# Row additions in pieces, closer search rounds, packed list operands, constant products between the waits, and ternary side work in later tiles

## The reference, cut to what matters

```
prob = softmax(z @ gate)              # layer 0: 2048 x 8
per expert: the 256 largest of prob[:, e]; x[tok] += tanh(g) * prob * expert(z[tok])
x += tanh(g) * shared(z)
```

## Time and profile before

| | |
|---|---|
| median of 3 executions | 921.93 us (921.6 to 922.6) |
| the profiled execution | 921.86 us, span 920.1 us |
| TensorE matmul busy | 835.7 us, 91% of the span |
| VectorE, ScalarE, GpSimd busy | 454.9, 325.4, 206.7 us |
| mean granted TensorE clock | 0.975 of full speed |

### The profile page before, as it was taken

The page is one execution under the profiler, slowest core; times in us unless marked ns, Lnnn a source line. Parts: engine busy times, 40 slices in busy tenths (PEclk is TensorE's granted clock), DMA queues, the critical chain, the costliest instruction groups (busy, mean ns, idle before and its releaser), DMA issues. The chain is left out here.

```text
span 920.1 us, 15092 instructions
## 1 busy us (share of the span) xinstructions
PE 835.7 (91%) x5798; PEld 646.3 (70%) x5806; DVE 454.9 (49%) x1240; ACT 325.4 (35%) x628; POOL 206.7 (22%) x226
## 2 busy tenths in 40 slices
PE   7899899999999997899999999888899996499996
PEld 5675665678888875666676667665677775388886
DVE  2674755400132317577676766755888776100000
ACT  2335022112322223555454545546455432122121
POOL 0123600020424310001000101111756124212222
PEclk9999899999999999999999999999999997599999
DMA  6032800014646447000000000000000002436351
GB/s 230 24 126 81 324 26 23 24 28 181 226 151 196 114 118 262 1 2 1 1 2 1 2 1 1 2 1 1 1 1 2 24 35 81 138 104 205 126 179 21
DMA packets 33873, 70.58 MB, mean 77 GB/s; under 512 B 9218, under 2 KB 23946, under 8 KB 28939
## 3 DMA queue, kind: packets, MB, share of 16 engines
q1 hardware_dynamic: 26937, 59.92, 18.2%
q0 software_dynamic: 6144, 8.31, 4.7%
q10 hardware_dynamic: 722, 1.39, 0.4%
HBM read 54.98 MB, written 14.80 MB: 76 GB/s over the span
## 5 line engine op out<-in xcount | busy, mean ns | idle before, releaser
L604 PE MATMUL banks<-arena 32*120 32x256 f32 (+6 forms) x1808 | 161.6, 377 | 15.9 <-DVE small L1965 12.6
L1262 ACT ACTIVATE arena<-banks 128x512 f32<-128x512 f32 (+4 forms) x185 | 106.8, 596 | 148.8 <-PE banks L1053 33.5
L604 PEld LDWEIGHTS banks<-arena 32*120 32x120 f32 (+5 forms) x1808 | 101.1, 163 | 51.7 <-issue 33.0
L604 PE MATMUL banks<-ffw,arena 128*128 128x256 bf16 (+2 forms) x632 | 120.0, 344 | 0.5 <-issue 0.2
L604 PE MATMUL banks<-arena,ew 128*128 128x256 f32 x512 | 115.6, 385 | 1.4 <-ACT arena L1262 1.4
L604 PE MATMUL banks<-ew,arena 128*128 128x256 f32 x512 | 113.2, 379 | 0.0
L604 PEld LDWEIGHTS banks<-arena,ew 128*128 128x128 f32 x512 | 98.9, 194 | 15.6 <-ACT arena L1262 2.0
L604 PEld LDWEIGHTS banks<-ew,arena 128*128 128x128 f32 x512 | 96.4, 190 | 12.3
L604 PEld LDWEIGHTS banks<-ffw,arena 128*128 128x128 f16 (+1 forms) x640 | 86.6, 138 | 25.2 <-issue 2.7
L1965 DVE TENSOR_REDUCE small<-banks 128x16 f32<-128x1920 f32 x32 | 69.0, 2157 | 20.8 <-PE banks L604 20.7
L1456 ACT ACTIVATE arena<-banks,mcol 120x2048 f32<-120x2048 f32 x32 | 63.1, 1971 | 19.0 <-PE banks L604 19.0
(11 more groups left out here) (242 smaller groups left out, 1237.4 us busy)
## 6 DMA issues: line engine op xcount, KB each, us to landing
ew<-in_w SPq DMA_DIRECT2D x32, 1024.0 KB, 7.1
xrow<-arena SPq DMA_DIRECT2D x1, 2064.0 KB, 22.0
arena<-xrow SPq DMA_DIRECT2D x8, 258.0 KB, 4.2
zrow<-arena SPq DMA_DIRECT2D x8, 256.0 KB, 2.2
ffw<-in_shared SPq DMA_DIRECT2D x2, 1024.0 KB, 6.0
acc<-x SPq DMA_DIRECT2D x4, 512.0 KB, 2.9
ffw<-in_tern SPq DMA_DIRECT2D x2, 1024.0 KB, 7.8
out<-x SPq DMA_DIRECT2D x8, 256.0 KB, 2.0
```

Source lines behind the costliest of these rows:

```text
L604: return pe.matmul(o, l, r, start=a, stop=b)
L1262: return nc.scalar.activation(o, i_, ACT.Copy)
```

## The change

- The bias row is added to `x` tile by tile, the addition of tile t after comparison t + 1; the later GpSimd work of `prepare_later` is cut and spread over rounds in the same way.
- Rounds are 4.5 units apart (30 + 9r // 2), and the list and its turn come two units later behind the last round.
- `hi1`, `lo1`, `lo2` and the digits are stored tile by tile, so that a tile's 128 columns lie side by side; the comparison with `iotaA` then repeats each digit as the innermost element. `add_shared(4)` comes behind the list's operands.
- `fill(bank, n)` issues n f32 products of 128 columns of a constant matrix of ones into a bank that is not in use: 15, 4 and 12 at the start, 6 in the first gate, 8, 14, 18 and 12 in the last gate, 40 and 22 behind its last ranks, the 22 after the moves have landed.
- The side steps of the last two batches move from ahead of the ternary tiles into tiles 4 to 10; GpSimd's `weigh` is split, and `weigh(1)` and `weigh(2)` come earlier.

The diff (context cut):

```
...
 XROW = D + 2
+FILL = {0: {0: 6}, 3: {5: 8, 6: 14, 7: 18}}
...
 def round_at(r):
-    return 30 + 5 * r
+    return 30 + 9 * r // 2
...
         c.at = 0
-        lo2 = c.take(16 * P, "p (m t) -> p m t", dt=F16, t=NT)
+        lo2 = c.take(16 * P, "p (t m) -> p t m", dt=F16, t=NT)
...
         c.at = 17344
-        iotaA = c.take(16 * NT, "p (a t) -> p a t", dt=F16, a=16)
+        iotaA = c.take(16, dt=F16)
...
         c.at = 18432
-        hi1 = c.take(16 * P, "p (m t) -> p m t", dt=F16, t=NT)
-        lo1 = c.take(16 * P, "p (m t) -> p m t", dt=F16, t=NT)
+        hi1 = c.take(16 * P, "p (t m) -> p t m", dt=F16, t=NT)
+        lo1 = c.take(16 * P, "p (t m) -> p t m", dt=F16, t=NT)
...
         posi = c.take(3 * P, "p (a n) -> p a n", dt=I32, a=3)
-        digit = c.take(2 * P, "p (a e t) -> p a e t", dt=F16, a=2, e=E)
+        digit = c.take(2 * P, "p (a t e) -> p a t e", dt=F16, a=2, e=E)
...
         su = sems("setup", "AB_ps AB_sb M_ps M_sb tanh gsum_in gsum_ps gsum_out pick16 parts later "
-                           "wT_ps wT_sb B_ps B_sb col_ps col_sb row_ps row_sb krow tern trow_ps trow_sb")
+                           "wT_ps wT_sb B_ps B_sb col_ps col_sb row_ps row_sb krow consts tern trow_ps trow_sb")
...
             g.memset(tri[:, :], 1.0)
-            g.drain()
+            g.drain().then_inc(su["consts"], 1)
...
                 g.drain().then_inc(su["later"], 1)
-                g.wait_ge(sh["cmp"], 1)
-                for i in range(T // 512):
-                    g.wait_ge(gt["z"], 2 * i + 2)
-                    xt = x[:, 4 * i:4 * i + 4, :]
-                    g.tensor_tensor(xt, xt, bcast(r, 1, 4), ALU.add).then_inc(su["later"], 1)
-                g.tensor_copy(iotaA[:, :, :], bcast(iota16[:, :], 2, NT))
+                for t in range(NT):
+                    g.wait_ge(sh["cmp"], t + 1)
+                    m = g.tensor_tensor(x[:, t, :], x[:, t, :], r, ALU.add)
+                    if t % 4 == 3:
+                        m.then_inc(su["later"], 1)
+                g.wait_ge(sh["cmp"], NT + 1)
+                g.tensor_copy(iotaA, iota16[:, :])
...
                 g.wait_ge(su["pick16"], 1)
-                g.tensor_copy(pick[:, :, :], bcast(pick16, 2, SK))
+                for a in range(4):
+                    g.wait_ge(sh["cmp"], NT + 2 + a)
+                    g.tensor_copy(pick[:, 4 * a:4 * a + 4, :], bcast(pick16[:, 4 * a:4 * a + 4], 2, SK))
...
                 for n, t_ in (("o1", 1), ("f1", 5), ("o2", 2)):
+                    g.wait_ge(sh["cmp"], NT + 6 + t_ // 2)
...
                     g.tensor_tensor(hw[:, t % 2], h2[:, t % 2], wrow, ALU.mult).then_inc(f2["hw"], 1)
+
+                def spread(t):
...
                 weigh(0)
-                rstd_side(UN - 1)
                 weigh(1)
-                add_bias(NB - 2)
+                spread(0)
                 weigh(2)
-                add_bias(NB - 1)
+                spread(1)
+                spread(2)
...
                     weigh(t)
+                    spread(t)
+                    if t == 5:
+                        rstd_side(UN - 1)
+                    elif t == 6:
+                        add_bias(NB - 2)
+                    elif t == 8:
+                        add_bias(NB - 1)
...
+            def fill(bank, n):
+
+                for _ in range(n):
+                    mm(bank[:, 0:P], onesf[:, :], onesf[:, :], True, True)
+
...
+            pe.wait_ge(su["consts"], 1)
+            fill(psum[7], 15)
...
                 turn_weights(psum[2 + a], n)
+            fill(psum[7], 4)
...
                 def gate_turn(k):
-                    pe.wait_ge(gt["z"], b0 + k + 1)
...
                         pe.wait_ge(gt["zT_sb"], b0 + k)
+                    fill(psum[6 if L == 0 else 2], FILL[L].get(k, 0))
+                    pe.wait_ge(gt["z"], b0 + k + 1)
...
                     w = t1 - t0
-                    pe.wait_ge(gt["picked"], n + 1)
...
                     pe.wait_ge(one["pT_sb"], b0 + (6 if n == 0 else NB))
+                    if n == 3:
+                        fill(psum[3], 12)
+                    pe.wait_ge(gt["picked"], n + 1)
...
                     if L == 0:
+                        fill(psum[7], 12)
                         pe.wait_ge(load["values"], 32)
-                    if L == 0:
...
                         group_ranks(3)
+                        fill(psum[3], 40)
+                        pe.wait_ge(gt["moved"], 16 * NT)
+                        fill(psum[3], 22)
...
                 for t in range(NT):
-                    m = mm(psum[7][:, 0:P], hi1[:, :, t], lo2[:, :, t], t == 0, t == NT - 1)
+                    m = mm(psum[7][:, 0:P], hi1[:, t, :], lo2[:, t, :], t == 0, t == NT - 1)
...
             between = {round_at(r): [lambda r=r: count(r)] for r in range(ROUNDS)}
-            for u, f in ((7, count_above), (16, rank_tokens), (36, list_tokens), (54, turn_list)):
+            for u, f in ((7, count_above), (16, rank_tokens), (38, list_tokens), (56, turn_list)):
...
                 tern_turn(0)
-                side_turn(UN - 2)
...
                     tern_out(t - 2)
-                    if t == 2:
+                    if t == 4:
+                        side_turn(UN - 2)
+                    elif t == 8:
...
                 take_high(0)
-                take_side(UN - 2)
...
                     take_high(t - 1)
-                    if t == 2:
+                    if t == 5:
+                        take_side(UN - 2)
+                    elif t == 9:
...
                 V.tensor_tensor(sel2, prob, tf, ALU.is_equal).then_inc(q["c_in"], 1)
-                add_shared(4)
...
                 for a in range(2):
-                    V.tensor_copy(digit[:, a, :, :], posi[:, 1 + a, :].rearrange("p (t e) -> p e t", t=NT))
+                    V.tensor_copy(digit[:, a, :, :], posi[:, 1 + a, :].rearrange("p (t e) -> p t e", t=NT))
...
                 for a, hot in ((1, lo1), (0, hi1)):
-                    V.tensor_tensor(hot.rearrange("p (e a) t -> p e a t", e=E), bcast(digit[:, a, :, :], 2, 16),
-                                    bcast(iotaA[:, :, :], 1, E), ALU.is_equal)
-                v.drain()
-                V.tensor_tensor(lo2, lo1, bcast(tokE, 1, P), ALU.mult).then_inc(q["hot"], 1)
+                    V.tensor_tensor(hot.rearrange("p t (e a) -> p t e a", e=E), bcast(digit[:, a, :, :], 3, 16),
+                                    bcast(bcast(iotaA, 1, E), 1, NT), ALU.is_equal)
+                v.drain()
+                V.tensor_tensor(lo2, lo1, bcast(tokE, 2, P), ALU.mult).then_inc(q["hot"], 1)
+                add_shared(4)
...
                 tern_stats(0)
-                side_stats(UN - 1)
...
                 tern_low(0)
-                side_low(UN - 2)
-                side_norm(UN - 1)
...
                 tern_low(1)
-                side_low(UN - 1)
...
                         tern_low(t - 1)
+                    if t == 4:
+                        side_stats(UN - 1)
+                    elif t == 6:
+                        side_low(UN - 2)
+                    elif t == 7:
+                        side_norm(UN - 1)
+                    elif t == 10:
+                        side_low(UN - 1)
...
```

## The result

The changed kernel takes **907.81 us**, the median of six executions (906.82 to 914.12), against 922.80 us (921.60 to 933.35, six executions) for the kernel before, run beside it: a ratio of 0.985, 95% interval 0.982 to 0.988. That is faster by 1.5%, and 2.1 us above the forecast of 905.7.

What follows compares the result with a forecast made beforehand. TensorE, busy for 91% of the span, was taken as the bound, losing time idle or at half clock. Gains 6.3 + 4.65 + 1.3 + 3.0 + 1.1 = 16.35, rounded to 16.2, from 921.9 gave 905.7 us; range 900.5 to 912.5.

Steps and rivals of the forecast that it cites:

- Row additions and the search: First search rounds: additions tile by tile end a 6.8 us loss on TensorE, less 0.5 for small waits; gain 6.3 us.
- list operands: Token list: packed operands cut the 16 products from 3.8 to 1.0 us and avoid a clock drop; gain 4.65 us.
- The distance of the rounds: Search: closer rounds by themselves give nothing, since the same 30 counts run and TensorE is never idle between them.
- Rival (b): Search: rounds now wait for VectorE, losing 0.25 us in each of 24, 6 us in all; 911 us, chance 0.14.
- Ternary tiles: First ternary tiles: the wait for GpSimd's weighting goes and the output runs at full clock; gain 3.0 us, bounds 1.0 and 3.9.
- Start: Kernel start: fills warm the clock, so the key row and first values come earlier; gain 1.3 us, bounds -0.5 and +2.3.
- about nine run cold and six warm: Start: of the 15 fills nine run at half clock, six at full, ending near 6.7, 1.8 us after `ident`.
- Last gate: Last gate and tail: experts begin 2.0 us later but warm, saving 0.6 and 2.5 us; net 1.1 us, bounds -1 and +4.
- Rival (d): All fills: they run cold at 0.45 us each and make the kernel slower; 932 us, chance 0.04.
- (a): Tail and start: fills fit better than priced, giving tail gain 4 and start gain 2; 901.5 us, chance 0.15.

Runs made afterwards that it cites:

- the experiment: The changed kernel with the order of the ternary part and its side work as before: 910.05 us, ratio 0.989 (0.984 to 0.993).

## Why the prediction was right, and where it was off

The stretches of the profile without the first gate give 10.63 + 3.02 + 0.26 = 13.9 us, and the forecast's base of 921.9 less that is 908.0, the median within 0.2 us. The miss of 2.1 us is mostly two terms of the sum: the start, which gave nothing of its 1.3, and the last gate, which gave 0.3 of its 1.1.

- **Row additions and the search** (6.3) and **list operands** (4.65): 10.95 forecast for the stretch, 10.63 measured. Alone, the additions gave 5.8 in the stretch and 6.7 between shortest executions, the list 5.3 in the stretch and 3.5 to 4.2 in the medians. The loss was also not one comparison alone: before, a second operation of VectorE in the same round (L1746, from 92.28) took 2.23 us beside the same additions. The list's products cost the 1.0 us that I took. An addition took 0.73 us, not the 0.58 of a quarter of 2.32, so there is a fixed part of some 0.2 us. It hid, as forecast: what it holds up is a small operation of VectorE ahead of TensorE's next count. VectorE's list operations rose by 3.2 us, as bounded, and fit with 0.4 us to spare; with another microsecond on VectorE the gain would have shrunk. The Trainium skill (VectorE: DVE Perf Modes, What auto-detection actually checks) gives the double rate only to operands with step one; 1.18 becoming 2.25 us per 2048 values agrees.
- **The distance of the rounds**: forecast to give nothing by itself, and rounds of five units gave 907.83. Rival (b) is out: no count waits more than 0.2 us.
- **Ternary tiles** (3.0): 3.02 in the trace; in the experiment 2.2 between medians, 3.0 between shortest executions and in the trace. Its parts agree too: the wait is 1.80 us, the transposes behind it come out 2.61 us earlier against 2.6 forecast, and 0.41 more behind them is the 0.85 of clock less the 0.44 of the turn moved there.
- **Start** (gain of 1.3): this step failed; in the profiled execution even its sign, -0.63. What failed first is "about nine run cold and six warm": 15 fills took 6.52 us, and the 12 took 4.20 of the at most 5 allowed. The "some 4 us" behind it did not follow from the rows that I gave: products resumed at 96.99 and the clock was still low up to 102, which is 5 us. In seven profiles with this start the 15 fills take 5.50 to 6.52 us. The base was off as well. These seven show the transposes of z at 18.30, 18.43, 18.56, 20.58, 20.69, 20.78 and 20.91, and six profiles without any fill at the start show them at 18.47, 18.57, 18.75, 20.28, 20.67 and 20.86; the 20.28 from which I counted the gain is one of the late ones. So both kinds of start come in an early and a late form about 2 us apart, the fills do not decide which, and their means are 19.8 and 19.6. I had also left out that the keys need `rows`, whose load ended at 15.2 to 17.3 in the kernels that waited for it.
- **Last gate** (net 1.1): 0.26 for gate and tail together. The mechanism was right and two of its sizes were off. Against the shift that the kernel already had (7.44 us at the turn of batch 4), TensorE began the experts 2.45 us later, not 2.0: the 62 fills took 14.1 us where I had 13.4 (0.227 us each, not 0.216), while the ranks came 0.8 us earlier, as forecast. And the clock gave back 2.78, not 3.1: from the first transposes to the end of the first expert half it is 8.46 us, where it was 11.24. The forecast also had the fills ending 3.1 us behind the rows' landing; the kernel without the 22 shows 3.3. It took that delay as given, and the better kernels come from cutting it. Against the kernel without any fill, the 114 fills of the last gate and behind it gave 0.5 us.
- **Not foreseen: the clock's fall in the first gate.** It took 5.6 us of the profiled execution. I had watched the clock where the change acts, and took the first gate as paced by VectorE and so indifferent. That the median came so near the forecast is in part luck: two of six executions are the long ones here, and with four it would have been some 5 us higher. The kernel with 8 fills at the start has four of six over 910 us. In the profiles with this start the fall is long (over 13 us) in two kernels, short (3 to 4 us) in three, and absent in two; in the four changed kernels without the start's fills it is absent, though one of their executions had a mean clock of 0.989. The list alone on the kernel before, which has the old start, shows it as well:

```profile
66.00:68.00 2.00, 1.49 (x6) 0.68 (x5) 1.05 (x6) 0.87 (x2) 0.69 (x1) 0.66 0.03 8
68.00:70.00 2.00, 2.00 (x10) 2.00 (x11) 0.60 (x3) 0.00 (x0) 0.00 (x0) 0.50 0.27 92
```

  So it does not need the new products or the start's fills. Nor do the gaps alone decide it: the kernel with rounds five units apart issues the same products 0.33 us earlier, is busy for the same 1.49 us from 68 to 70, and stays at 1.00. What decides whether the fall comes in an execution stays open.
- **Rival (d)** is half true: the fills do run cold at the start. They end 3 us after `ident` has landed, but what follows runs warm, so that the key row is ready at 15.2 where it was 17.0; and in the last gate the fills are warm, at 0.23 us each.
- Two sums of the rivals are off by little: (a) adds 2.9 and 0.7 us to the forecast's gain, which gives 902.1 and not 901.5, and (b) gives 911.7, not 911.

## What to carry to other kernels

Filler work in front of a wait should be shorter than the shortest form of that wait: here an overshoot of 3.3 us cost 3.3 us, and the clock that the filler saves was worth 2.3 to 2.8 us, once. A GpSimd operation that stretches VectorE's did less harm in pieces, each placed where VectorE has only small steps left. A stretch with small gaps is where the clock fell in some executions and not in others, so compare executions of one kernel, or the stretch alone in both traces, before giving a difference of five microseconds to an edit. And a base taken from one profile may be the late form of something that comes in two.

## What the runs showed of the hardware

- The granted clock is shown as 1.00 in the first 10 us, while 15 constant f32 products take 6.52 us there and 5.50 to 6.38 us in six other kernels with the same start. So the rise comes at a different point from one execution to the next.
- Constant products do raise and hold the clock: behind 15 of them the first transposes take 0.60 us, where they took 1.11. Behind 40 of them, 9.18 us, and a wait of 1.25, 1.50 or 1.78 us the expert half takes 7.17 us; behind the same 40 and a wait of 1.51 or 3.03 us it took 8.86, after 10.46 us of idleness 9.47.
- A GpSimd addition of two f32 operands took 2.32 us for 1024 columns and 0.73 for 256. A VectorE operation of 0.17 us beside the latter took 0.68.
- 16 products of f16 operands with a step of 16 elements took 3.98 us, side by side 1.06.
- With identical code, executions of the changed kernel differ by 7 us. A fall of the clock for over 13 us in the first gate cost 5.5 us in three profiles, one of 3 to 4 us cost 0.9 in three.
- The rows were asked for 2.5 to 3.0 us after the start of the last move in twelve profiles, but 3.7 and 4.3 us after it in two.
